# One-hot look-ups, base scales and late loads of a graph network kernel, sent and awaited at other places

## What is computed

```python
h = jnp.maximum(_layernorm(x), 0.0)
weight = jnp.einsum('rb,bio->rio', w_comp, bases)      # 32 relations, 8 bases of 512x512
msg = (jnp.einsum('ni,rio->rno', h, weight))[etype, src] * norm
x = x + segment_sum(msg, dst) + h_bias                  # first layer
h = jnp.maximum(_layernorm(x), 0.0)
h = h @ W.T + b                                         # second layer, self loops added
x = x + relu(segment_sum(dis[row] * dis[col] * h[row], col))
```

## Time and profile before

| | |
|---|---|
| three runs | 627.3, 627.65, 631.69 us (median 627.65) |
| profiled execution, first to last instruction | 625.8 us |
| busy: PE, DVE, ACT, POOL | 496.4, 328.6, 151.9, 352.2 us |
| set-up until PE's first slot | about 64 us |
| PE's 335 slots | about 64 to 545 us |
| second layer behind the slots | 545 to 625.8 us |

### The profile page before, as it was taken

How to read it: one execution, slowest core, us unless ns; L and a number is a source line. 1 busy time by engine, 2 the same in 40 slices (tenths; PEclk the granted TensorE clock), 3 DMA queues, 4 the chain that set the end, 5 groups by cost and what they waited for, 6 DMA issues and landing times.

```text
span 625.8 us, 15841 instructions
## 1 busy us (share of the span) xinstructions
PE 496.4 (79%) x5824; PEld 317.0 (51%) x5824; DVE 328.6 (52%) x929; ACT 151.9 (24%) x272; POOL 352.2 (56%) x473
## 2 busy tenths in 40 slices
PE   3031445598999899999999998999897876889996
PEld 1020334356666556666656665566564554545443
DVE  7898038885665446636655556645542221544121
ACT  3392234532222122211322202203210000341021
POOL 3334536786676776766747757677677777200000
PEclk9665657599999999999999999999997977789999
DMA  9896965557786887886858868778788788323042
GB/s 283 306 362 216 391 161 150 166 152 211 217 278 202 255 259 205 256 262 175 272 153 252 258 189 262 222 235 273 210 250 261 216 234 240 118 68 102 2 98 68
DMA packets 53427, 132.82 MB, mean 212 GB/s; under 512 B 12173, under 2 KB 18174, under 8 KB 53350
## 3 DMA queue, kind: packets, MB, share of 16 engines
q0 software_dynamic: 27040, 99.60, 53.1%
q1 hardware_dynamic: 25356, 30.99, 15.9%
q10 hardware_dynamic: 954, 1.13, 0.6%
HBM read 120.58 MB, written 11.10 MB: 210 GB/s over the span
## 4 chain that ended last, share of the span: by engine, by line
PE 52%; DMA 14%; DVE 12%; issue 8%; ACT 5%; POOL 5%; SPq 3%; ACTq 1%; POOLq 0%; DVEq 0%
PE PS L1521 22%; PE PS L1501 16%; DMA gath<-rows_layer,srcs 9%; PE PS L1595 7%; POOL gath L722 5%; PE PS L1541 4%; DMA types<-types_by_slot 2%; SPq L579 2%; DVE room_b L1225 2%; ACT room_b L841 2%; DVE zt L1225 1%; DMA edge_records<-room_c 1%; DVE room_b L1261 1%; DMA w1t<-edge_records,w1t 1%; PE PS L1507 1%
## 5 line engine op out<-in xcount | busy, mean ns | idle before, releaser
L722 POOL DMA_INDIRECT gath<-rows_layer,srcs x335 | 335.7, 1002 | 165.1 <-issue 84.8
L1501 PE MATMUL PS<-sel,gath 128*128 128x48 f16 (+7 forms) x4020 | 299.1, 207 | 52.8 <-DMA gath<-rows_layer,srcs 21.8
L1501 PEld LDWEIGHTS PS<-sel,gath 128*128 128x128 f16 x4020 | 235.4, 103 | 163.9 <-issue 86.6
L1521 PE MATMUL PS<-room_b,zt 128*128 128x512 f16 x480 | 168.6, 392 | 1.5 <-DVE sel L1147 1.0
L1521 PE MATMUL PS<-room_b 128*128 128x512 f16 (+1 forms) x480 | 151.7, 384 | 2.0 <-DMA gath<-rows_layer,srcs 1.8
L1141 DVE TENSOR_TENSOR masks<-iota_n,dloc 128x24 bf16<-128x24 f32 (+12 forms) x92 | 17.9, 194 | 96.6 <-issue 58.8
L1507 PE MATMUL PS<-oh_ad,gath 128*128 128x30 bf16 (+7 forms) x335 | 65.1, 194 | 0.0
L782 ACT CAST val<-val_f 128x64 f16<-128x64 f32 x42 | 11.0, 262 | 201.8 <-DVE val_f L1098 196.8
L1521 PEld LDWEIGHTS PS<-room_b 128*128 128x128 f16 (+1 forms) x480 | 47.8, 105 | 16.8 <-DMA gath<-rows_layer,srcs 2.1
L1521 PEld LDWEIGHTS PS<-room_b,zt 128*128 128x128 f16 x480 | 45.2, 100 | 8.6 <-issue 2.2
L1147 DVE TENSOR_TENSOR sel<-masks,val 128x192 f32<-128x192 bf16 (+12 forms) x92 | 38.6, 420 | 0.0
(11 more groups left out here) (202 smaller groups left out, 409.9 us busy)
## 6 DMA issues: line engine op xcount, KB each, us to landing
room_b<-in_L_gnn_bases_dram SPq DMA_DIRECT2D x8, 1024.0 KB, 9.3
gath<-rows_layer,srcs POOLq DMA_INDIRECT x335
types<-types_by_slot SPq DMA_DIRECT2D x168, 16.0 KB
x_t<-x_base SPq DMA_DIRECT2D x19, 128.0 KB
u_t<-in_x_dram SPq DMA_DIRECT2D x9, 256.0 KB, 6.2
x_base<-u_t SPq DMA_DIRECT2D x9, 256.0 KB
x_layer<-x_t SPq DMA_DIRECT2D x18, 128.0 KB
u_t<-x_layer SPq DMA_DIRECT2D x18, 128.0 KB, 2.7
```

The lines of the kernel that those rows point to most:

```text
L722: pool.indirect_dma_start(out=gath[:, s % UN, :], out_offset=None, in_=tab0_d[:, :], in_offset=bass.IndirectOffsetOnAxis(ap=srcs[:, s:s + ...
L1501: mm(there, gath[:, s % UN, D * t + P * f:D * t + P * (f + 1)], sel_parts[:, here, k, 0:NB * w, u], start=first and t == 0 and u == 1, sto ...
L1521: last = mm(PS[0:r, PBANK[q], :], zt[q % 2][:, t, f, b, 0:r], base_hl[:, b, u, f, :], start=(m == 0), stop=(m == NM - 1))
```

## The change

- Low parts: GpSimd makes all ten; DVE's three go.
- Types of groups 3 to 5 are sent by SP directly behind groups 1 and 2, ahead of bases 5 to 7. They were sent behind W1. Each still waits for the one-hot of the group three before.
- W1 is sent by ACT, behind the set-up's values and a wait for all low parts, no longer by SP behind the biases and the landed table.
- One-hots of groups 3 and on move from step 8v-23 to 8v-15, look-ups from 8v-18 to 8v-12. Group 3: from steps 1 and 6 to 9 and 12.
- `largest` and `scale` move from steps 7 and 8 to 13 and 14, base splits from 10 + 3n to 15 + 3n.

```diff
-        LOWS, BEARLY = 7, 5
+        BEARLY = 5
-        SQ_SETUP, SC_AT, BS_AT, WT_AT = BEARLY, 7, 10, 38
+        SQ_SETUP, SC_AT, BS_AT, WT_AT = BEARLY, 13, 15, 38
...
-            STEPS[VB * v - 23].append(("types", v))
-            STEPS[VB * v - 18].append(("look", v))
+            STEPS[VB * v - 15].append(("types", v))
+            STEPS[VB * v - 12].append(("look", v))
...
-                if i < LOWS:
-                    sp.wait_ge(s_h0lo_pool, i + 1)
-                else:
-                    sp.wait_ge(s_h0lo, i - LOWS + 1)
+                sp.wait_ge(s_h0lo, i + 1)
...
-            for v in range(1, TRING):
+            for v in range(1, TRING + VEARLY):
                 load_types(v)
             for n in range(BEARLY, NB):
                 load_base(n)
...
-            sp.wait_ge(s_tab0, 16 * (NT + 3))
-            sp.dma_start(w_in, W1.rearrange("(c p) i -> p c i", p=P)).then_inc(s_win, 16)
             sp.wait_ge(s_xbase, 16 * NT)
-            for v in range(TRING, TRING + VEARLY):
-                load_types(v)
...
-            for i in range(LOWS):
+            for i in range(NT):
                 pool.wait_ge(s_h0hi, i + 1)
...
+            act.wait_ge(s_h0lo, NT)
+            act.dma_start(w_in, W1.rearrange("(c p) i -> p c i", p=P)).then_inc(s_win, 16)
...
-            for i in range(LOWS, NT):
-                low(i)
```

More of the change, by code:

```diff
@@ L414, in gnn_kernel @@
         s_h0lo = sem("s_h0lo")
-        s_h0lo_pool = sem("s_h0lo_pool")
         s_tab0 = sem("s_tab0")
@@ L696, in _ @@
                     in_offset=bass.IndirectOffsetOnAxis(ap=offs[:, c:c + 1], axis=0)).then_inc(s_padr, 16)
-            for i in range(LOWS):
+            for i in range(NT):
                 pool.wait_ge(s_h0hi, i + 1)
                 t = table_of(i)
-                g.tensor_tensor(t[:, 1, :], x_in[0:XROWS[i], i, :], t[:, 0, :], ALU.subtract).then_inc(s_h0lo_pool, 1)
+                g.tensor_tensor(t[:, 1, :], x_in[0:XROWS[i], i, :], t[:, 0, :], ALU.subtract).then_inc(s_h0lo, 1)
             pool.wait_ge(s_tab0, 16 * (NT + 3))
@@ L999, in _ @@
                 v.tensor_copy(typ16[:, c, :], padr[:, c, :, 2]).then_inc(s_loc, 1)
[L1001 to L1004, removed]
             def columns_max(n):
```

## The result

The changed kernel takes 633.79 us (median of four runs; 632.39 to 635.95), the kernel before 627.91 us on the same chip. The ratio is 1.0084, with a 95% interval of 1.0053 to 1.0114: 0.5 to 1.1% slower. The prediction said 620.5 us and a range up to 626.5; it was wrong, and on the wrong side.

A forecast was written before the change was run, and what follows sets the result against it. The prediction took PE's stalls before its second half tile, on late one-hots and base splits, as what the change touches: 625.8 - 13.2 + 6.1 = 618.7, with 1.85 us for the median 620.5 us, 1.1% faster; range 615.0 to 626.5.

The forecast's parts named there:

- What is late next: ACT's squares: First flush waits for ACT's four squares: last landing near 80.4, ACT free at 82.5, PE's second half tile at 83.8.
- T1: Moment PE's second half tile begins, after the first flush: 97.00 before, forecast 83.8, 13.2 us earlier (bounds 82.2 to 88.5).
- 1.9 us shorter: DVE's set-up list, less three low parts given to GpSimd; so no time was taken for the types' waits for one-hots.
- 4.8 us "against": Before the first flush: gathers no longer pause, so six more (1.8 MB) can go, delaying the landing 4.8 us.
- The 5.4 us "for": Before the first flush: biases (0.5 MB) no longer ahead of W1 and 1.5 MB of gathers already through, together 5.4 us.
- The first rival: Transfers only swap places on full DMA engines: last landing 85.1, T1 88.5, 625.2 us, no change; chance 0.26.
- The second rival: Two queues beat the gathers, getting two thirds of 369 GB/s: T1 79.3, 616.1 us; chance 0.15.
- The third rival: Slower: shorter lead makes PE wait for DVE at each later look-up; 634 us at 0.37 us each; chance 0.07.
- T3: Moment PE's third half tile begins, after the third flush; 137.90 in the kernel before.
- The price behind T1: DVE work moved behind the first flush: net loss 6.1 us, bounds 0.2 to 8.9.
- my 7.1 us of moved work: On DVE behind the first flush: group 3's value and the scales, 4.8, plus one more base split, 2.3.
- The 1.0 us that I let return: At look-up 7, which now comes behind the turns of W1, where PE had waited 1.98 us: 1.0 us back.

The follow-up runs named there:

- the doses: Changed kernel with types of groups 3 to 5, of group 3 alone, or of none ahead of bases 5 to 7: 633.79, 625.81, 621.31 us.
- u_bases: Changed kernel, but SP sends bases 5 to 7 ahead of the types of groups 3 to 5: 621.31 us, ratio to the kernel before 0.9838.
- after: The changed kernel itself, with all parts of the change, against the kernel before: 633.79 us, ratio 1.0084.
- a_hold: Changed kernel, but GpSimd holds gather 13 and all behind it until the squares are done: 627.9 us, ratio to the kernel before 0.9979.
- b_steps: Kernel before with only the later steps of one-hots, look-ups, scales and base splits: 629.72 us, ratio 1.0014.
- u_steps: Changed kernel with one-hots, look-ups, scales and base splits at their old steps, loads as changed: 634.0 us, ratio to the kernel before 1.0075.
- b_types: Kernel before with only the types of groups 3 to 5 sent ahead of bases 5 to 7: 633.09 us, ratio 1.0074.
- u_w1sp: Changed kernel, but W1 sent by SP again, behind the biases and the landed table: 633.72 us, ratio to the kernel before 1.0039.
- the second measurement: Changed kernel with the types of groups 3 to 5 behind bases 5 to 7, measured again in more runs: 621.09 us, ratio to the kernel before 0.9851.

## Why the prediction was wrong, point by point

**The step that failed** is "What is late next: ACT's squares". It named the right engine and the right four instructions. It put the landing of the last megabyte near 80.4, between 76.7 and 85.1; it was 89.1. With it T1, forecast 83.8 and 88.5 at the latest, was 94.76. The landing is 8.7 us late, and what follows it adds 2.2 of the 11.0 us at T1 (5 below). Points 1 to 4 are the terms that were wrong; they overlap and are no sum:

1. *When the bases leave.* I had 55.8 us, from an earlier end of the table's writing, twelve issues and no wait for the one-hots. The table's writing did end early (47.98; forecast 46.8). But the twelve transfers cannot leave before the one-hots of groups 0 to 2, at 52.28, 54.13 and 56.31, and DVE's set-up did not get shorter. I had written that the list was "1.9 us shorter" without asking what GpSimd's extra work does to DVE. 2.6 us of error, which by the doses (2.1 us each) are about 5.4 us at the flush.
2. *What 1 us of leaving costs.* I charged it as 1 us. The doses say 2.1. Part of the 14.1 us between u_bases and after is queue time lost while the engines were half empty, 4.0 us from the bytes moved by 64 us; 5.8 us are the eight gathers that get in ahead (a_hold). The bytes from 50 us to base 7's square say nearly the same: u_bases moves 8.15 MB in 25.01 us (326 GB/s), after 11.66 MB in 39.12 (298). The 3.5 MB more are 9.1 us at 385 GB/s, 2.4 MB of them the eight gathers, and 5.0 us are engines that were not full. This is an estimate from two profiles; it leaves some 1.1 MB, 3 us, that I cannot name.
3. *The gathers.* I had them in the sum as 4.8 us "against", set off against 5.4 us for biases and early gathers. a_hold puts them at 5.8 us, and b_steps, u_steps and b_types agree in sign (W1 3.7 us later without the stall, base 7 6.1 and 6.7 us earlier with it). The pause of the gathers in the kernel before was worth something: while PE waited, the megabytes came in.
4. *The 5.4 us "for" were hardly there.* 1.5 MB of gathers were to be through early. By 58.36 us GpSimd had begun five gathers, before four: 0.3 MB, 0.8 us at 369 GB/s. The forecast start itself, 3.8 us earlier, was worth only three gathers, 0.9 MB. And the 0.5 MB of biases was credited to W1, but base 7 came last, and the biases had always stood behind it.
5. *Behind the landing.* I had one square to do after it, 2.1 us. It was base 7 that came last, with W1's square queued behind its own: 89.12 to 93.12, 4.0 us; from there to PE 1.64 us, not 1.3. Together 2.2 us, and 8.7 + 2.2 are the 11 us but for rounding.

**W1 in a third queue** was no gain at the flush (u_w1sp). The Trainium skill, "DMA: Bandwidth & Descriptors", section "Rules for kernel authors", says that spreading transfers over issuing engines gains no bandwidth, only issue time. The trace agrees: from 64 to 77.3 us the engines moved 385 GB/s with three queues, and 391 before. The first rival, which is that rule's outcome, came nearest of the three in its mechanism, but its landing of 85.1 was still 4 us early, since it took the bases' leaving from the same step.

**The second rival** fell. Two queues did not get two thirds of the engines. From 63.8 to 77.3 us GpSimd issued ten gathers, 2.95 MB or some 218 GB/s of 385 (an estimate, since they land later than they are issued); SP's and ACT's queues shared the other 167. The gathers kept their pace of 1.25 us until 72.55, when they began to wait for PE:

```profile
64.00:77.30 13.30, 8.76 (x112) 7.85 (x111) 1.60 (x7) 2.00 (x2) 9.12 (x10) 0.50 1.04 385
```

The Trainium skill, "DMA: Bandwidth & Descriptors", section "Queues, rings and completion order", has each DMA engine take turns, packet by packet, between the queues that have work. The trace shows no even split of bytes between the three.

**The third rival** fell too. Its 634 us are the measured time, but that is luck: PE's waits for a one-hot are seven in the whole run, 12.9 us, and 12.7 of these lie between 46 and 150 us; behind T3 the two kernels take 487.8 and 487.9 us. No cost of the later look-ups shows in the long part.

**What held.** The 13.40 us gap went, and the thirteen slots ran to 81.1 (forecast 78). The price behind T1 was 7.1 us where I took 6.1, and every kernel with the new steps has it, from 46.5 to 48.0 us against 40.9, whatever its loads. It comes mostly at its end: of the 7.1 us, 0.7 lie between the first and second flush's end (94.76 to 116.85; 97.00 to 118.35 before) and 6.3 between the second and third. There DVE has five base splits, three before, and the last stands at 138.13, right ahead of the third flush. DVE's busy time from T1 to T3 grew by 5.8 us and its idle time by 1.3, so that my 7.1 us of moved work is right as a sum and in part by luck. The clock that TensorE was granted is not the cause: from the first to the second flush's end it was 0.66 in b_types and u_steps, which have the old price, and 0.66 in b_steps, which has the new one. The 1.0 us that I let return did not.

```profile
137.08 0.28 DVE L1074 TENSOR_SCALAR oh_t<-types,rel 128x256 bf16<-128x256 bf16 x1
...
138.13 2.35 DVE L1248 SCALAR_TENSOR_TENSOR room_b<-room_b,scale_i 128x2048 f16<-128x2048 f32 x1
```

The first gather, forecast 50.5, came at 52.46, 1.90 us behind `flag` at 50.56, as it does in u_bases (50.25, 52.15), not behind the table. So the change holds a gain and a loss. With the bases in front, the gain ahead of T1 is 16 us (97.00 to 80.94) for 7 us behind it. Not all of the 9 us between shows in its profile, since behind T3 it takes 492.5 us there and 490.7 in the second measurement; over all the profiles that part varies from 487.8 to 492.5, with no pattern that I could tie to an edit. The medians, 1.2 to 1.8% lower, are what the claim of a better version rests on.

## What to carry to other kernels

When small transfers are put ahead of large ones in one queue, count not their bytes but the waits and issues that stand in front of the large ones, and ask what else will use the engines meanwhile: here 6.7 us of leaving became 14 us of landing. Taking away a stall also takes away the pause in which other transfers came in, so the next wait must be worked out with the traffic that the stall held back. Send the large transfers first while the DMA engines are half idle, and let those that wait for a semaphore stand behind them.

## What the runs showed of the hardware

- Late megabytes can cost more than their lateness: 2.1 us at the flush for each us at SP in three kernels that differ only in the place of the types (51.69, 54.46 and 58.36 against 79.01, 84.94 and 93.12).
- Gathers keep their pace beside full queues: some 218 of 385 GB/s up to 77.3 us, while SP's and ACT's queues, with the rest of five megabytes to send (three bases, W1, biases, rows of x), had 167.
- GpSimd's 128x512 subtractions slow some of DVE's small instructions: three casts 2.57 us beside them and 0.63 without, a 12x12 operation 0.82 and 0.22, but a reduction 0.27 and 0.27. The Trainium skill, "GPSIMD Engine Reference", section "1. Specifications", states that GpSimd's interfaces to SBUF are shared with VectorE, and that they contend with VectorE's instructions in a two-port mode or with two inputs in SBUF. The trace agrees that the two disturb each other, and has the price; which mode the casts ran in it does not show.
